# Narrow matmuls one piece to a chunk, a banded convolution matrix, x quantised on GpSimd

## The reference, cut to what matters

```python
# layer 0: x (8, 128, 512); a gate per (image b, row e), from the mean over the first length[b] columns
y    = einsum('bet,bt->be', x, mask) / length
gate = sigmoid(conv1d(y, conv_w))                       # 5 taps along the 128 rows, padding 2
h    = bitlinear(silu(bitlinear(x * gate, w_gate)) * bitlinear(x * gate, w_up), w_down)
x    = x + h       # bitlinear: the input rounded to 8 bits per row, the weight to -1, 0, 1 times its mean |w|
# layer 1: a weight made from a codebook, and experts of low rank chosen by a softmax
w_eff = quantised(weight + lora_delta) + lora_delta
c = x @ w_eff.T
x = x + c @ W_base.T + b_base + sum_e alpha_e * (c @ A_e.T) @ B_e.T * 2    # alpha from router logits of c
```

## Time and profile before

| | |
|---|---|
| median of three runs | 167.55 us |
| the profiled execution | 166.95 us |
| its span, first to last instruction | 165.2 us |
| TensorE matmul busy | 151.2 us, 92% |
| VectorE busy | 114.5 us, 69% |
| ScalarE busy | 99.7 us, 60% |
| GpSimd busy | 5.7 us, 3% |
| mean granted TensorE clock | 0.959 |

### The profile page before, as it was taken

How to read it: one execution, slowest core, us unless ns; L and a number is a source line. 1 busy time by engine, 2 the same in 40 slices (tenths; PEclk the granted TensorE clock), 3 DMA queues, 4 the chain that set the end, 5 groups by cost and what they waited for, 6 DMA issues and landing times.

```text
span 165.2 us, 2369 instructions
## 1 busy us (share of the span) xinstructions
PE 151.2 (92%) x775; PEld 94.6 (57%) x782; DVE 114.5 (69%) x308; ACT 99.7 (60%) x169; POOL 5.7 (3%) x25
## 2 busy tenths in 40 slices
PE   7889999976899999974997899999999999999993
PEld 2266575823367478531662365555557667688783
DVE  2799999789799489569948747798988311107362
ACT  3899998974996677299565355868663420320200
POOL 7000000000000000001000000000000000000000
PEclk9999999999997598799999689999999999999999
DMA  5999999298000000000000000000000000000093
GB/s 181 375 416 417 419 404 391 81 346 309 0 0 0 4 2 0 0 0 0 4 0 0 0 0 4 2 0 0 2 4 0 0 0 0 4 0 0 0 375 133
DMA packets 6543, 15.99 MB, mean 97 GB/s; under 512 B 658, under 2 KB 914, under 8 KB 6532
## 3 DMA queue, kind: packets, MB, share of 16 engines
q1 hardware_dynamic: 6532, 15.85, 25.3%
HBM read 13.76 MB, written 2.10 MB: 96 GB/s over the span
## 4 chain that ended last, share of the span: by engine, by line
PE 70%; ACT 14%; DVE 10%; issue 5%; ACTq 0%; DVEq 0%
PE bank L895 13%; PE bank L808 11%; PE bank L814 11%; PE bank L842 9%; ACT tern_d L475 6%; PE bank L827 3%; PE bank L853 2%; PE bank L669 2%; ACT tern_i L505 2%; PE bank L749 2%; PE bank L666 2%; PE bank L726 2%; PE bank L902 1%; PE bank L741 1%; PE bank L782 1%
## 5 line engine op out<-in xcount | busy, mean ns | idle before, releaser
L808 PE MATMUL bank<-tern_g,head_sb 128*128 128x464 bf16 (+1 forms) x96 | 25.6, 394 | 0.7 <-DVE tern_u L1110 0.7
L814 PE MATMUL bank<-tern_u,head_sb 128*128 128x464 bf16 (+1 forms) x96 | 25.5, 393 | 0.0
L1222 DVE TENSOR_TENSOR raw_up<-bank,wbt 128x464 f32<-128x464 f32 (+1 forms) x24 | 15.2, 632 | 12.9 <-ACT wbt L568 9.2
L842 PE MATMUL bank<-tern_d,delta 128*128 128x512 bf16 (+1 forms) x81 | 19.2, 380 | 3.4 <-DVE tern_d L1110 3.0
L895 PE MATMUL bank<-m_h,fr 128*128 128x512 f32 (+1 forms) x72 | 22.1, 375 | 0.0
L568 ACT ACTIVATE wbt<-bank,s_g 128x464 f32<-128x464 f32 (+1 forms) x24 | 15.3, 641 | 3.6 <-PE bank L808 3.5
L726 PE MATMUL bank<-wbt,cond 128*128 128x512 f32 x32 | 15.0, 603 | 2.6 <-DVE cond L1042 2.6
L575 ACT ACTIVATE raw_up<-raw_up,hq 128x1376 int16<-128x1376 f32 x8 | 11.5, 1441 | 8.9 <-DVE hq L1232 8.9
L814 PEld LDWEIGHTS bank<-tern_u,head_sb 128*128 128x128 bf16 x96 | 10.2, 107 | 11.6 <-issue 3.5
L842 PEld LDWEIGHTS bank<-tern_d,delta 128*128 128x128 bf16 (+1 forms) x88 | 8.4, 98 | 13.2 <-DVE tern_d L1110 4.0
L1225 DVE TENSOR_REDUCE hmax<-raw_up 128x1 f32<-128x464 f32 (+1 forms) x24 | 15.1, 631 | 0.8
(11 more groups left out here) (173 smaller groups left out, 241.5 us busy)
## 6 DMA issues: line engine op xcount, KB each, us to landing
raw_gate<-in_w_gate_t SPq DMA_DIRECT2D x4, 688.0 KB, 7.9
raw_up<-in_w_up_t SPq DMA_DIRECT2D x4, 688.0 KB, 12.9
xs<-in_x SPq DMA_DIRECT2D x8, 256.0 KB, 13.4
out_x<-xs SPq DMA_DIRECT2D x7, 256.0 KB, 2.2
raw_down<-in_w_down_t SPq DMA_DIRECT2D x2, 768.0 KB, 5.4
cond<-in_cond_w SPq DMA_DIRECT2D x4, 256.0 KB, 4.5
wbt<-in_w_base_t SPq DMA_DIRECT2D x4, 256.0 KB, 9.9
raw_down<-in_w_down_t SPq DMA_DIRECT2D x2, 512.0 KB, 7.7
```

The source lines that it names most:

```text
L808: mm = pe.matmul(bank_g[n % 2][:, 0:w], xq_t[:, b % 2, k, :], tern_g[:, k, f0:f0 + w], start=(k == 0), stop=(k == KH - 1))
L814: mm = pe.matmul(bank_u[n % 2][:, 0:w], xq_t[:, b % 2, k, :], tern_u[:, k, f0:f0 + w], start=(k == 0), stop=(k == KH - 1))
L842: mm = pe.matmul(bank_down[:], h_t[0:rows, b % 2, j, :], tern_d[0:rows, j, :], start=(j == 0), stop=(j == KF - 1))
L1222: dve.tensor_tensor(hs, bank_u[n % 2][:, 0:w], silu[:, n % 2, 0:w], ALU.mult)\
```

## The change

- The convolution is one matmul with a banded matrix (band) that GpSimd builds from the shifted identities and the taps in nine instructions, once all masks are made. conv(0) waits for it. VectorE's y_taps becomes y_mean.
- x_quantise of images 2 to 7 moves from VectorE to GpSimd.
- On VectorE, value(3), w_eff(3) and weight_scale(1) stand ahead of the second ternary chunk, and x_max(0, 2) behind y_safe(0).
- selection, last_fold and weight_total(2) stand one or two pieces to a chunk over images 0 to 3; b_rows moves to image 0; x1_transposes(0) moves from between the chunks of image 3 to behind its last one.
- The last group's gates: conv(2) goes with x_transposes(3) instead of (4), y_safe(2) to image 2, gates(2) and x_scales(5, 8) to the first chunk of image 3.
- On ScalarE the rounding of up's last chunk, the sums of |w_down| and the copies of b and m_s move to match. The hidden rows lie in the gate weights' buffer instead of the up weights', and M the other way round (not in the diff below).

```diff
--- before.py
+++ after.py
@@ -60,7 +61,7 @@
 GROUPS = [(0, 2), (2, 5), (5, NB)]
-CONV_WITH_XT = {1: 1, 4: 2}
+CONV_WITH_XT = {1: 1, 3: 2}
 TINY_SQUARE = 1e-36
...
@@ -95,15 +96,15 @@
         bank_m = [bank[0], bank[1], bank[2], bank[3]]
-        bank_ms = bank[2]
+        bank_ms = bank[3][:, SEL_END:SEL_END + KH * ZL]
         bank_delta = [bank[2], bank[3], bank[6], bank[7]]
         bank_sel = bank[3]
-        bank_b = bank[3]
+        bank_b = bank[2]
         conv0 = (HT_LATE * P + H) // 2
...
-        bank_total = [bank[7][:, 0:KH], bank[7][:, 0:KH], bank[3][:, 0:len(DOWN_PARTS)]]
+        bank_total = [bank[7][:, 0:KH], bank[7][:, 0:KH], bank[2][:, 0:len(DOWN_PARTS)]]
         bank_warm = bank[4]
...
@@ -191,7 +192,8 @@
         ymean = sb("ymean", [P, NB])
-        ytaps = sb("ytaps", [P, TAPS, NB])
+        band = sb("band", [P, P])
+        band_part = sb("band_part", [P, P])
         ycond = sb("ycond", [P, NB])
...
@@ -420,10 +424,34 @@
+            pool.wait_ge(ld_head, 16)
+            pool.wait_ge(ident_done, 1)
+            pool.wait_ge(mask_done, NT * KH)
+            pool.tensor_scalar(band[:], shifts[:, 0:P], cw[:, 0:1], None, ALU.mult).then_inc(band_done, 1)
+            for i in range(1, TAPS):
+                pool.wait_ge(band_done, 2 * i - 1)
+                pool.tensor_scalar(band_part[:], shifts[:, i:i + P], cw[:, i:i + 1], None, ALU.mult)\
+                    .then_inc(band_done, 1)
+                pool.wait_ge(band_done, 2 * i)
+                pool.tensor_tensor(band[:], band[:], band_part[:], ALU.add).then_inc(band_done, 1)
+
+            def x_quantise(b):
+                pool.wait_ge(qx_done, 2 if b < GROUPS[2][0] else 3)
+                pool.wait_ge(xt_ps, b - 1)
+                pool.tensor_scalar(xq_i[:, b % 2, :], xs[:, b, :], gate[:, b:b + 1], qx[:, b:b + 1],
+                                   ALU.mult, ALU.mult).then_inc(xq_pool_done, 1)
+
+            def residual_scale(b):
+                pool.wait_ge(hscale_done, b + 1)
+                pool.tensor_scalar(s_d[:, b:b + 1], harow[:, b:b + 1], w127[:, 2:3], None, ALU.mult).then_inc(sd_done, 1)
+
+            x_quantise(2)
+            x_quantise(3)
             pool.wait_ge(winv_done, 3)
             for b in range(NB):
-                pool.wait_ge(hscale_done, b + 1)
-                pool.tensor_scalar(s_d[:, b:b + 1], harow[:, b:b + 1], w127[:, 2:3], None, ALU.mult).then_inc(sd_done, 1)
+                residual_scale(b)
+                if b + 4 < NB:
+                    x_quantise(b + 4)
...
@@ -525,6 +553,8 @@
                 act.wait_ge(fold_ps, k + 1)
+                if k == 0:
+                    act.wait_ge(tern_out, 2 * NC - 1)
                 act.activation(m_full[:, k, :], bank_m[k][:], ACT.Copy).then_inc(mfull_done, 1)
...
@@ -543,7 +573,6 @@
             rounded_chunk(1, 1)
-            rounded_chunk(1, 2)
...
@@ -598,50 +627,56 @@
             for b in range(NB + 3):
+                if b == 3:
+                    gate_silu(2)
                 if b < NB:
                     silu_chunk(b, 0)
-                if b >= 3:
+                if b >= 4:
                     x1_high(b - 3)
+                if b == 0:
+                    rounded_chunk(1, 2)
                 if b == 1:
                     gate_silu(1)
-                    weight_sum_down(2)
+                    act.wait_ge(b_ps, 1)
+                    act.wait_ge(rows_done, 5)
+                    act.activation(b_full[0:3 * ZC, :], bank_b[0:3 * ZC, :], ACT.Copy,
+                                   scale=two_row[0:3 * ZC, :]).then_inc(b_full_done, 1)
+                    weight_sum_down(1)
                 if b == 2:
-                    act.wait_ge(ms_ps, 1)
-                    act.activation(ms_h, bank_ms[:, 0:KH * ZL].rearrange("p (k c) -> p k c", k=KH),
-                                   ACT.Copy).then_inc(msh_done, 1)
                     rounded_down(0)
...
                 if b == 0:
-                    weight_sum_down(0)
                     for k in range(KH):
                         m_copy(k)
+                if b == 1:
+                    weight_sum_down(2)
+                if b == 3:
+                    act.wait_ge(ms_ps, 1)
+                    act.activation(ms_h, bank_ms.rearrange("p (k c) -> p k c", k=KH),
+                                   ACT.Copy).then_inc(msh_done, 1)
                 if 1 <= b <= NB:
                     hidden_evacuate(b - 1)
+                if b == 2:
+                    rounded_down(2)
                 if 1 <= b < NB - 1:
...
                         conv_out(CONV_WITH_XT[b + 1])
-                if b == 2:
-                    rounded_down(2)
                 if b < NB:
...
                     conv_out(1)
-                    weight_sum_down(1)
+                    weight_sum_down(0)
                 if b == 1:
...
                     rounded_down(4)
-                    act.wait_ge(b_ps, 1)
-                    act.wait_ge(rows_done, 5)
-                    act.activation(b_full[0:3 * ZC, :], bank_b[0:3 * ZC, :], ACT.Copy,
-                                   scale=two_row[0:3 * ZC, :]).then_inc(b_full_done, 1)
                 if b == 3:
-                    gate_silu(2)
+                    x1_high(0)
                 if b in (5, 6):
...
@@ -683,7 +718,7 @@
                 else:
-                    pe.wait_ge(sel_read, 2)
+                    pe.wait_ge(b_full_done, 1)
                 pe.matmul(dst, ones[:], wsum[:, i, 0:parts], start=True, stop=True).then_inc(wtot_ps, 1)
...
@@ -729,18 +764,19 @@
             def b_rows():
-                pe.wait_ge(wtot_read, 3)
+                pe.wait_ge(mfull_done, 3)
+                pe.wait_ge(sel_done, 2)
+                pe.wait_ge(ld_exp, 32)
                 pe.matmul(bank_b[0:3 * ZC, :], sel_er[:], l1b, start=True, stop=True).then_inc(b_ps, 1)
...
                 if g == 0:
+                    pe.wait_ge(band_done, 2 * TAPS - 1)
                     pe.wait_ge(delta_done, KH)
                 b0, b1 = GROUPS[g]
-                for i in range(TAPS):
-                    mm = pe.matmul(bank_conv[g][:, 0:b1 - b0], shifts[:, i:i + P], ytaps[:, i, b0:b1],
-                                   start=(i == 0), stop=(i == TAPS - 1))
-                mm.then_inc(conv_ps, 1)
+                pe.matmul(bank_conv[g][:, 0:b1 - b0], band[:], ymean[:, b0:b1], start=True,
+                          stop=True).then_inc(conv_ps, 1)
...
@@ -768,7 +804,7 @@
             def x_transposes(b):
-                pe.wait_ge(xq_done, b + 1)
+                pe.wait_ge(*((xq_done, b + 1) if b < 2 else (xq_pool_done, b - 1)))
                 pe.wait_ge(ident_done, 2)
...
@@ -830,7 +866,7 @@
                 if b == 0:
-                    pe.wait_ge(msl_done, 1)
+                    pe.wait_ge(wtot_read, 3)
                 else:
...
@@ -846,7 +882,7 @@
                 if b == 0:
-                    pe.wait_ge(b_full_done, 1)
+                    pe.wait_ge(msl_done, 1)
                 else:
...
@@ -907,27 +943,40 @@
                 gate_up(b, 0)
-                if b >= 3:
+                if b == 0:
+                    fold(KH - 1, 2)
+                if b == 1:
+                    selection(0)
+                    selection(1)
+                if b == 2:
+                    weight_total(2, bank_total[2], len(DOWN_PARTS))
+                    last_fold(0)
+                if b == 3:
+                    last_fold(3)
+                if b >= 4:
                     x1_transposes(b - 3)
...
                 if b == 0:
-                    fold(KH - 1, 2)
                     fold(KH - 1, 3)
+                if b == 1:
+                    selection(2)
+                    selection(3)
+                if b == 2:
+                    last_fold(1)
                 if b >= 1:
...
                     x_transposes(b + 1)
-                if b == 2:
-                    b_rows()
                 gate_up(b, 2)
...
                     x_transposes(1)
-                    for k in range(KH + 1):
-                        selection(k)
+                    b_rows()
                 if b == 1:
-                    for k in range(KH):
-                        last_fold(k)
-                    weight_total(2, bank_total[2], len(DOWN_PARTS))
+                    selection(KH)
+                if b == 2:
+                    last_fold(2)
+                if b == 3:
+                    x1_transposes(0)
                 if b >= 2:
...
@@ -1065,11 +1114,9 @@
-            def y_taps(g):
-                b0, b1 = GROUPS[g]
-                link(dve.tensor_tensor(ymean[:, b0:b1], ysum[:, b0:b1], len_r[:, b0:b1], ALU.mult))
-                dve.tensor_tensor(ytaps[:, :, b0:b1], ymean[:, b0:b1].unsqueeze(1).broadcast_to([P, TAPS, b1 - b0]),
-                                  cw.unsqueeze(2).broadcast_to([P, TAPS, b1 - b0]), ALU.mult).then_inc(ymean_done, 1)
+            def y_mean(g):
+                o = slice(*GROUPS[g])
```

(55 more changed lines are left out.)

11 lines of the change are left out of this document (7 added, 4 removed).

## The result

Over 20 runs each on the same chips the changed kernel takes 167.71 us (median) and the kernel before 167.12; the ratio is 1.007, 95% interval 1.0036 to 1.0104. The ratio leaves out executions more than 1.5% above the fastest of the same kernel, which before has (up to 170.28) and after has not, while over all 20 the medians differ by 0.35%: that the forecast gain is not there is clear, that the loss is as much as 0.7% is less so. The forecast was 165.05, a gain. The profiled execution of after takes 166.66 us, before's 166.95.

A forecast was written before the change was run, and what follows sets the result against it. TensorE bounds from gate_up(5, 0); before it, VectorE's order, waits and half clock. After gate_up(0, 0), 54.2 us against 59.66 saves 5.5, less 3.0 for clock: 2.5 off 166.95 gives 164.45, median 165.05; range 161.0 to 169.0.

The forecast's parts named there:

- Conv(0)'s matmul near 33: Head: conv(0) waits for GpSimd's band, out at 33.1; a start before 31.5 or after 34.5 refutes the step.
- band's term: GpSimd's nine 128-column instructions after the last mask: 4.7 us with hand-overs, plus 1.0 beside VectorE; bounds 2.5 and 10.6.
- The row that I leaned on: Head: s_d at 77.53, 0.50 beside VectorE against 0.28 alone, cited against GpSimd being fully shut out.
- Gate_up(0, 0) at 40.6, no gain and no loss: End of head: the w_eff(3) wait of 2.55 us goes, waits for band and x_quantise(0) replace it; 40.59 before.
- (D): Rival, chance 0.19: VectorE shuts GpSimd out, band out at 35.6, clock falls, folds lose 3.4, gate_up(0, 0) 45.3; 169.5 us.
- From there to gate_up(5, 0) 54.2 us and twice 1.5 for the clock, 57.2: Gate_up(0, 0) to gate_up(5, 0): 12.3 + 6.2 + 2.0 + 16.2 + 17.5 us, against 59.66, plus two half-clock stretches.
- The wait ahead of x_transposes(2): TensorE waits about 4 us, near 55 to 59, for GpSimd's x_quantise(2); 1.5 us more if the clock falls.
- the second fall that I had counted: Gate_up(3, 0) behind down(0): clock 0.50 after two waits of about 1.5 and 2.7 us, costing 1.5 us.
- The last wait and the last loss of clock: Before gate_up(5, 0): the 2.03 us wait for x1 and the half clock after it go.
- The sum: Whole kernel: 5.5 us saved after gate_up(0, 0), 3.0 lost to clock, 2.5 saved; 164.45 profiled, median 165.05.
- (C): Rival, chance 0.22: GpSimd slower in band and x_quantise(2) (1.8 us); 166.5 us, spreading narrow matmuls does nothing for the time.

The follow-up runs named there:

- e1_taps: The changed kernel without band: old convolution by taps on VectorE and five shifted matmuls, no wait for band; ratio 0.9733 to the kernel before, median 163.22 us.
- e11_before_gates: The kernel before with only the last group's conv(2), y_safe(2), gates(2) and x_scales(5, 8) sooner; ratio 0.9859 to the kernel before.
- e10: The kernel before with only VectorE's new head order (value(3), w_eff(3) ahead of the second ternary, x_max behind y_safe); ratio 0.9858 to the kernel before.
- e3: The kernel before with only the banded convolution, band built on GpSimd behind the last mask; ratio 1.0023 to the kernel before.
- e7: The changed kernel with the old taps convolution and the narrow matmuls back in two runs; ratio 0.9794 to the kernel before, median 163.09 us.

## Why the prediction was wrong, point by point

**Conv(0)'s matmul near 33: it came at 35.07.** This is the step that failed: band's term, 4.7 us alone and 1.0 for VectorE beside it. Measured it is 7.4 us (27.59 to 34.97). A tensor_scalar of 128 columns takes 0.60 alone (the one at 33.83, VectorE idle) and not 0.46, a tensor_tensor 0.45 as taken; five and four of them with eight hand-overs of 0.09 make 5.6, where I had 4.7. Beside VectorE's x_sum, ternary and w_eff the same tensor_scalar took 0.91 to 1.16, and one tensor_tensor 0.64: 1.8 us in all, where I had put 1.0. GpSimd also began 0.2 later than taken. So band came 1.9 us late: 0.9 by the price of the nine alone, 0.8 by the price beside VectorE, 0.2 by the start. The row that I leaned on, s_d with 0.22 of delay, was one of the mildest cases. Everything queued behind conv(0) moved with it.

**Gate_up(0, 0) at 40.6, no gain and no loss: it came at 42.70.** From band to there my working held: 7.7 us, forecast 7.5; VectorE's part from the total (35.95) to the end of x_quantise(0) (41.13) is 5.2, forecast 5.3. Last to come was TensorE: the ten records of the folds took 5.96 us, where e1_taps has 4.54, and let x_transposes(0) start at 41.57, 0.4 behind x_quantise(0). So the whole error of 2.1 us at this mark is band's 1.9, and some 0.2 of clock. It lay between the forecast and rival (D), which had band at 35.6.

**From there to gate_up(5, 0) 54.2 us and twice 1.5 for the clock, 57.2: measured 56.80.** The sum came out by luck: two of its parts are wrong by nearly 2 us each, the opposite ways. To hq(0) it took 12.3 us (forecast 12.3), to the end of x_quantise(2) 5.6 (6.2), to the end of gate_up(1, 2) 3.7 (3.5 with the clock), to the end of down(0) 18.0 (16.2), to gate_up(5, 0) 17.2 (19.0 with the clock). The wait ahead of x_transposes(2) is there (3.31 us, forecast 4), and the clock is 0.50 behind it as said, but through three gate_ups and not one; the second fall that I had counted, in gate_up(3, 0) behind down(0), did not come. GpSimd's x_quantise takes 0.77, forecast 1.2; VectorE's takes 0.55. The last wait and the last loss of clock are gone as forecast, and e11_before_gates gives 1.4% for it.

**The sum.** 0.4 us too much behind gate_up(0, 0), 2.1 too little ahead of it: 0.6 us saved at gate_up(5, 0) and not 2.5, and 0.3 in the executions' own times. The runs say that not even this is left. What made it: the change holds two parts worth 1.4% each alone (e10, e11), and one wait that costs 3.4% where it stands (after against e1_taps). That a wait takes the place of w_eff(3)'s I had right in kind, and e3 shows it. I then counted it as no gain from w_eff(3) and no loss; but without it 1.7 us of gain in the head were there to be had (gate_up(0, 0) at 38.91 in e1_taps and e10), and with it gate_up(0, 0) came 2.1 later than before.

**The rivals.** (D)'s mechanism is what happened, and band at 34.97 is past the 34.5 from which I had said it decides, but at half its price: gate_up(0, 0) 2.1 us late and not 4.7, with 1.4 us of clock in the folds and not 3.4. The Trainium skill (SBUF — State Buffer, section SBUF: two separate sides) has the loser of the shared port pair fully blocked for the other's whole instruction. The trace agrees in kind and not in size: band's second instruction lay beside all of one x_sum (0.75) and 0.35 us of the next and grew by 0.56 over 0.60, while neither x_sum grew; over all nine, some 2.9 us beside w_eff, x_sum and ternary cost 1.8. The measurement decides: about two thirds of a full block. Value(3), with one operand in PSUM, did not hold band up at all (0.45 at 31.61 in after, as alone). (C)'s slow x_quantise did not occur; its claim that the spread does nothing for the time the runs can't refute (e7).

**Left open.** The ratio of after to e1_taps is 3.4%, 5.6 us, while their medians differ by 4.5 and their profiled executions by 4.3. The runs of each are spread over 2.4 and 3.6 us, so the size of the wait's price is known to about 1 us. Why the clock stayed at 0.50 through three gate_ups in after and through one in e1_taps, behind waits of 3.31 and 3.04 us, no run shows.

## What to carry to other kernels

Where a change takes work off one engine by giving a preparation to another, look first at what is queued behind the wait on the preparation, and start the preparation where nobody waits: here the same matrix cost 3.4% waited for, and 1.1% (built early, on the masks) or nothing (used from the second group on) where nobody waited, of which the 1.1% can't be told from nothing. When a wait is removed from the path, any wait that stood in its shadow becomes the path, so parts that are free alone must be priced again together. Waits that the clock or another engine hides show up in full only when the cover is gone, and the one filler tried kept the clock and only moved the wait.
